# Moving the old pair's last mixes and its second mean square within a step of a software-pipelined state-space mixer

## What is computed

```python
proj = x @ Win.T                       # x_ssm, z, Bm, Cm, dt_raw; 32 heads, P=64, N=128
dt = softplus(dt_raw + dt_bias)
xc, Bc, Cc = (silu(causal_conv(u, w)) for u, w in ...)   # 4 taps
decay = exp(dt * -exp(A_log)); dtx = dt[..., None] * xc
h = decay * h + dtx[..., None] * B[:, :, None, :]        # scan over 256 tokens
y = einsum('bhpn,bhn->bhp', h, C)
y = y * rsqrt(mean(y * y, axis=-1) + 1e-6)
y = y * silu(z)
return y.reshape(B, T, H * P) @ Wout.T
```

## Time and profile before

| | before |
|---|---|
| median of 3 runs | 677.91 us |
| profiled execution: span from first to last instruction | 680.0 us |
| PE busy | 636.0 us, 94% |
| DVE busy | 531.8 us, 78% |
| ACT busy | 447.2 us, 66% |
| POOL busy | 475.5 us, 70% |

### The profile page before, as it was taken

One profiled execution on the slowest core, in us unless ns is written; L12 is line 12 of the kernel. 1 busy time (PEld: TensorE's weight loads), 2 busy tenths in 40 slices (PEclk: granted clock), 3 DMA queues, 4 the chain that ended last, 5 costly groups with the idle time before them and its releaser, 6 DMA issues.

```text
span 680.0 us, 11968 instructions
## 1 busy us (share of the span) xinstructions
PE 636.0 (94%) x3544; PEld 493.4 (73%) x3544; DVE 531.8 (78%) x849; ACT 447.2 (66%) x723; POOL 475.5 (70%) x452
## 2 busy tenths in 40 slices
PE   7999999999999999999999999999999999899920
PEld 6677887888878878888788788788898776455510
DVE  6999999999999999999999999859754539222236
ACT  3768788788787887887878879875324445333321
POOL 5395988789879887798798887586805817655244
PEclk9999999999999999999999999999999969999965
DMA  4231113113111131121111311133062780587324
GB/s 157 107 134 48 65 47 109 62 47 109 58 50 62 47 109 62 47 105 53 59 62 47 109 62 46 37 96 107 24 171 78 190 329 4 169 257 200 88 89 128
DMA packets 25896, 65.08 MB, mean 96 GB/s; under 512 B 4051, under 2 KB 16851, under 8 KB 23131
## 3 DMA queue, kind: packets, MB, share of 16 engines
q1 hardware_dynamic: 23035, 56.96, 25.2%
q0 software_dynamic: 2832, 7.75, 4.4%
HBM read 56.42 MB, written 8.28 MB: 95 GB/s over the span
## 4 chain that ended last, share of the span: by engine, by line
PE 68%; DVE 15%; issue 6%; ACT 5%; POOL 4%; DMA 2%; POOLq 0%; DVEq 0%; ACTq 0%
PE ps L835 27%; DVE conv L1662 8%; PE ps L865 7%; PE ps L849 5%; PE ps L1129 5%; PE ps L767 3%; PE ps L785 3%; ACT decay L1330 3%; PE ps L1173 3%; DVE decay L1646 3%; PE ps L850 2%; PE ps L809 2%; POOL conv L706 2%; PE ps L1103 1%; PE ps L874 1%
## 5 line engine op out<-in xcount | busy, mean ns | idle before, releaser
L1662 DVE SCALAR_TENSOR_TENSOR conv<-ps,w_raw,conv 128x506 f32<-128x506 f32 (+3 forms) x352 | 320.9, 935 | 12.1 <-ACT conv L1324 7.2
L835 PE MATMUL ps<-x_hi,w_hi 128*128 128x512 f32 x384 | 158.1, 412 | 3.8 <-DVE conv L1662 2.0
L835 PE MATMUL ps<-x_hi,w_lo 128*128 128x512 f32 x384 | 151.1, 393 | 0.0
L835 PE MATMUL ps<-x_lo,w_hi 128*128 128x512 f32 x384 | 150.0, 391 | 0.0
L1324 ACT ACTIVATE conv<-ps,w_raw 128x512 f32<-128x512 f32 x160 | 108.1, 686 | 61.4 <-PE ps L835 61.2
L498 POOL TENSOR_TENSOR decay<-cum_b,cum_tok 128x512 f32<-128x512 f32 (+1 forms) x128 | 103.2, 828 | 9.0 <-DMA cum_b<-cum_scratch 9.0
L835 PEld LDWEIGHTS ps<-x_hi,w_hi 128*128 128x128 f32 x384 | 72.2, 188 | 21.4 <-DVE conv L1662 3.5
L504 POOL TENSOR_TENSOR decay<-decay,mask 128x512 f32<-128x512 f32 x64 | 82.4, 1288 | 5.0
L835 PEld LDWEIGHTS ps<-x_hi,w_lo 128*128 128x128 f32 x384 | 72.0, 188 | 16.8 <-DVE w_lo L1588 0.2
L849 PE MATMUL ps<-conv 128*128 128x256 f32 x256 | 79.6, 393 | 2.3 <-DVE xs L1637 0.4
L835 PEld LDWEIGHTS ps<-x_lo,w_hi 128*128 128x128 f32 x384 | 72.4, 189 | 12.7
(11 more groups left out here) (263 smaller groups left out, 1101.6 us busy)
## 6 DMA issues: line engine op xcount, KB each, us to landing
cum_b<-cum_scratch SPq DMA_DIRECT2D x16, 1024.0 KB, 4.7
w_raw<-in_winT SPq DMA_DIRECT2D x15, 778.0 KB, 4.3
y_all<-in_wgu SPq DMA_DIRECT2D x4, 1408.0 KB, 11.6
late<-in_wdn SPq DMA_DIRECT2D x2, 1408.0 KB
x_scratch<-conv SPq DMA_DIRECT2D x19, 128.0 KB, 4.6
late<-in_woutT SPq DMA_DIRECT2D x1, 2048.0 KB, 8.3
ys_scratch<-y_blk SPq DMA_DIRECT2D x32, 64.0 KB
res_scratch<-conv SPq DMA_DIRECT2D x11, 130.0 KB
```

Source lines behind the costliest of these rows:

```text
L835: mm = pe.matmul(ps[:, tile_bank(n, tile) + hf, :], wp[:, par, w], xp[:, kk, t], start=(i == 0), stop=(i == 5))
L1662: dve.scalar_tensor_tensor(out=o[:, :, s:], in0=u[:, :, 0:T - s], scalar=w_raw[:, par, c:c + 1], in1=o[:, :, s:], op0=ALU.mult, op1=ALU.ad ...
```

## The change

On PE, `mix(r, 2)` and `mix(r, 3)` go from behind unit 1 to behind unit 3 (after the second `x_to_tokens`), and `mean_square(r, 1)` goes from behind unit 3 to behind unit 6 (after `score(2)`). On ACT, the table change stays in `work[1]` but nothing stands ahead of it there any more, the squares of r's second half follow `rsqrt(r, 0)` behind copy 3, and `rsqrt(r, 1)` goes from behind copy 6 to behind copy 7. On DVE, `gate(r, rp, 1)` goes from ahead of tap (1,0) to ahead of tap (1,2). On POOL, `norm(r, 0)` changes places with `low_part(r, 1)`. Nothing is added or removed.

```diff
@@ POOL, step
                 if tail:
+                    norm(n - 2, par, 0)
                     low_part(n - 2, 1)
-                    norm(n - 2, par, 0)
@@ PE, between_tiles
-                    if tail and j == 1:
+                    if tail and j == 3:
                         mix(r, 2)
                         mix(r, 3)
-                    if tail and j == 3:
-                        mean_square(r, 1)
                     if mid:
                         for k in {4: (0, 1), 6: (2,), 7: (3, 4), 9: (5, 6)}.get(j, ()):
                             score(k)
+                    if tail and j == 6:
+                        mean_square(r, 1)
@@ ACT, work
                 if tail:
-                    work[1] += [lambda: square(r, 1)]
-                    work[3] += [lambda: rsqrt(r, 0)]
+                    work[3] += [lambda: rsqrt(r, 0), lambda: square(r, 1)]
                 if mid:
                     work[1] += [lambda: act.preload_act_table_set("natural_log_exp_and_others")]
...
                 if tail:
-                    work[6] += [lambda: rsqrt(r, 1)]
+                    work[7] += [lambda: rsqrt(r, 1)]
@@ DVE, step
-                if tail:
-                    between.setdefault((1, 0), []).append(lambda: gate(r, rp, 1))
                 if mid:
                     between.setdefault((1, 0), []).append(lambda: x_scaled(1))
+                if tail:
+                    between.setdefault((1, 2), []).append(lambda: gate(r, rp, 1))
+                if mid:
```

## The result

The changed kernel takes 699.27 us (median of 4 runs, 697.96 to 700.16) against 678.09 us for the kernel before in the same comparison: a ratio of 1.031 (95% interval 1.028 to 1.034), slower by 21.2 us. The forecast was 701.7 us, range 694 to 708.

The account below looks back on a forecast made before the run. PE was taken to bound the step, DVE close behind; 1.3 + 0.55 - 0.3 + 0.1 = +1.7 us per step, times 14 steps = 23.8 us, on the median 677.9 gives 701.7 us, range 694 to 708.

Parts of the forecast that it names:

- The bound: Steady step: PE bounds it, DVE follows closely; PE can gain at most about 0.3 us and lose any amount.
- The new wait: DVE at x_scaled(0): waits for the moved mixes, starting at 228.53 instead of 226.03, a new wait of 2.5 us.
- DVE's chain: DVE from x_scaled(0) to the end of tap (1,2): pieces sum to 5.82 us, ending at 234.35 instead of 232.81.
- Unit 6 and around: PE at unit 6: starts 1.3 us late, stalls 1.9 us; with mean square, score wait and restart, +1.7 us per step.
- Score 4's wait: PE before score 4: the 0.3 us wait for DVE's weighing 2 mostly goes, counted as -0.3 us per step.
- The profiled spans: Whole profiled execution: would go from 680.0 to 703.8 us, starting 0.3% over the median.
- Rival 1: DVE's waits of 0.9 and 0.5 us absorb part: 1.1 us per step, 693 us; chance 12%.
- Rival 2: Score 4 and tile 1's first tap: earlier table change removes PE's 0.3 us wait, none new, 673.7 us; chance 5%.
- Rival 3: PE's stall in each step drops TensorE's clock from 2.4 to 1.2 GHz for a part: 759 us; chance 3%.
- The parts costed at nothing: ACT's table change, squares and Ln/Exp, POOL's swap, exponents' wait, DMAs, steps 0, 1, 16, 17: covered or unchanged, no cost.
- POOL's swap: POOL: product starts near 228.8, low_part ends near 231.2; free, with 4.5 us idle per step.
- The mean square's cover: PE's mean square 1 wants POOL's low part only after 236: cover 5 us, otherwise PE would wait there.

Follow-up runs that it names:

- e2: Changed kernel with x_scaled waiting only for mixes reading its own half of xs, and x_scaled(1) one tap later, ahead of tap (1,1): 672.69 us, ratio 0.993.
- e6: Kernel before with only PE's part of the change (mixes behind unit 3, mean square behind unit 6): 725.62 us, ratio 1.071.
- e1: Changed kernel with x_scaled(c) waiting only for the mixes that read its own half of xs: 682.18 us, ratio 1.010.
- e9: Changed kernel with the second mean square directly behind the moved mixes, ahead of unit 4: 779.36 us, ratio 1.149.
- e10: e2 with POOL's order as in the kernel before (low_part ahead of norm): 673.10 us, ratio 0.992.
- e5: Changed kernel with the two mixes back behind unit 1, the rest of the change kept: 683.55 us, ratio 1.009.
- e4: Changed kernel with the gate ahead of tap (2,0) instead of (1,2): 700.49 us, ratio 1.034.
- e3: Changed kernel with x_scaled(0) behind tap (0,5), directly before x_scaled(1), its wait unchanged: 689.50 us, ratio 1.018.

## Why the prediction was right

The forecast was 701.7 us and the time is 699.27: the direction, the wait that causes the loss and the place where it shows came as forecast, and the cost per step was put 0.14 us too high.

**The bound.** PE and DVE in a loop, with PE able to gain 0.3 us: e2 shows the floor, 26.95 us per step, 0.35 under before.

**The new wait.** 2.5 us was forecast at x_scaled(0) and 2.54 measured. Its start was put 8.53 us into the step (228.53 - 220.00); it is 8.66. Units 2 and 3 were taken at 2.75 us from a pair that follows another unit; behind the transposes the first matmul is slower, and they take 2.86.

**DVE's chain.** The sum of the pieces was 5.82 us, measured 5.70 (180.68 to 186.38). The piece that shrank is tap (1,1), 1.19 to the next start where 1.31 was taken, because the gate now follows it and not a tap. Tap (1,2) was to end 14.35 us into the step and ends at 14.36; unit 6 starts at 14.41, forecast 14.4. That this hits to 0.01 us is luck: the start 0.13 too early and the chain 0.12 too long cancel.

**Unit 6 and around.** The later start, 1.3 us, came out. The stall did not: 1.9 us was forecast and 1.5 is lost. PE was to be ready the whole 0.55 us of the mean square sooner; but unit 4 behind the mixes has a slow first matmul, and score 1 starts at 182.77 where its pace would have it at about 182.6, since x_scaled(1) ends only at 182.63 (in e6 this wait is on record, as 0.60 us for DVE's xs). The two take 0.4 us out of the stall, and nothing out of the time. From there to the next step's start the change adds 0.22 us (14.45 against 14.23), where the terms gave 0.55 - 0.3 + 0.1 = 0.35. The mis-sized term is the mean square: its 0.55 us in the earlier trace rows held the slow first matmul behind a switch. Between a score and unit 7 that switch is paid either way, so the move adds about two matmuls at 0.23, that is 0.46. Score 4's wait gave back 0.35 and not 0.3. Hence 1.56 us per step; the terms as forecast add up to 1.65, which was rounded up to 1.7. The 4.7 us in which DVE was to reach weighing 2 behind tap (1,2) is nearly right by the end of weighing 2 alone (4.5 us behind the tap's end, 4.0 to its start).

**The profiled spans.** 703.8 was forecast for the span, and 696.6 came out. The steps account for +21.8 us; the rest, -5.2, lies in the stage of the experts. The same part of that stage by stretch, before and after:

```profile
545.00:575.00 30.00, 29.41 (x163) 21.74 (x161) 19.38 (x68) 14.20 (x41) 13.68 (x17) 0.83 0.45 178
```

```profile
565.50:592.00 26.50, 25.93 (x171) 19.50 (x170) 20.05 (x71) 15.65 (x43) 13.35 (x17) 1.00 0.57 224
```

Its 70 transposes of the hidden activations (line 1150) run, in the kernel before and then in the changed one:

```profile
L1150 PE MATMUL ps<-ident,h_tok x70: 270/273/421, 544.7 to 649.4; 128*88 128x128 f32 x70
```

```profile
L1150 PE MATMUL ps<-ident,h_tok x70: 270/273/311, 567.0 to 665.9; 128*88 128x128 f32 x70
```

That is 104.7 us against 98.9. The mean clock of 0.83 over 30 us is 10.2 us at the half clock, which costs half of that, 5.1 us; the other execution has none there. The slowest transpose took 421 ns, and 311 in the other. The 2.1 us by which the span of before was said to lie over the median set a span against a time; time against time it is about 4. The forecast started from the median and is not touched by it. A single profiled execution can carry that, so the medians, not the spans, give the change's size.

**The rivals.** Rival 1 (DVE's slack takes in a part) is out: DVE's 0.5 us wait for the first copy is still there, since it moves with PE. Rival 2 (faster) was two edits away: it needed x_scaled(0) not to wait for the moved mixes. The narrower wait of e1 is that, but alone it leaves the step at 27.64; together with x_scaled(1) one tap later it turns the loss into a gain (e2). Rival 3 (the clock) did not happen in this kernel; e6 and e9 show that it was near. The evidence against it, step 1 of the kernel before at 1.00 around waits of up to 1.1 us, is weaker than it looked: in e10 the clock fell in that very step, whose second wait was 1.55 us there.

**The parts costed at nothing.** POOL's swap: confirmed by e10. The mean square's cover of 5 us, for POOL's low part, is there: that ends at 183.40, and the mean square starts at 188.49. What the prediction did not name is that the mean square also waits for the gate, done at 185.72, so its real cover is 2.8 us; e9 takes it away, and PE stands 5.4 us for the gate. ACT's copies 2 and 3 came 1.7 us sooner, not 1.2, which changed nothing. The moves on ACT, DVE and POOL together are what keeps the change from losing 48 us (e6). The gate was in the sum only as a piece of the chain; with the mixes back in their place it is in the 0.48 us that are left (e5), with the mean square.

## What to carry to other kernels

When work on one engine is moved later, look for every wait that counts it, also those that hold by far today: here a guard on a shared tile, 0.6 us early before, became the head of a 5.7 us chain. Before moving producers, narrow such a guard to what it protects; a count of all mixes stood for four of eight blocks, which cost nothing until the order changed and 16 us afterwards. Where two engines each wait for the other once in a step, follow the loop around once: a stall can be shortened without a gain (e4), and what stands behind the wait counts in full (e3).

## What was not expected of the hardware

The clock fell in the mixer itself, in variants of the kernel whose waits are a little longer. With 2.1 us before unit 6 (and 0.6 us a little earlier) the granted clock fell to 0.50 in e6, in every third step at the same waits, and such a step took 31.7 us instead of 30.2. With 1.4 us, in the changed kernel, it stayed at 1.00 through the mixer. That is no bound: in e10 it fell once behind waits of 1.09 and 1.55 us, where e2 with the same waits kept it, and the step took 1.3 us more. A wait can thus bring a second loss on top, 7.5 us of the 48 in e6, and one execution can have it where another has not. Why one step falls and the next does not was not tried apart.
